# Beginning the transfers of the maxima rows from ScalarE's queue instead of SyncE's, in a two-layer fp32 transformer stack

## The reference, cut to what matters

```
x = x + attention_0(layernorm(x))   # ring attention: 16 heads of width 16, key blocks of 256
x = x + ffn(layernorm(x))           # ternary weights, relu squared
x = x + attention_1(layernorm(x))   # ordinary softmax attention, 16 heads of width 16
x = x + trees(layernorm(x))         # 8 decision trees of depth 7
```

## Time and profile before

| | |
|---|---|
| median of 3 runs | 3680.61 us (3670.45 to 3684.01) |
| the profiled execution | 3678.47 us |
| its span, first to last instruction | 3676.6 us |
| TensorE busy | 3089.0 us, 84% |
| VectorE busy | 2319.5 us, 63% |
| ScalarE busy | 1945.2 us, 53% |
| GpSimd busy | 885.4 us, 24% |
| mean granted TensorE clock | 0.914 of full speed |

### The profile page before, as it was taken

One profiled execution on the slowest core, in us unless ns is written; L12 is line 12 of the kernel. 1 busy time (PEld: TensorE's weight loads), 2 busy tenths in 40 slices (PEclk: granted clock), 3 DMA queues, 4 the chain that ended last, 5 costly groups with the idle time before them and its releaser, 6 DMA issues.

```text
span 3676.6 us, 58730 instructions
## 1 busy us (share of the span) xinstructions
PE 3089.0 (84%) x19068; PEld 1381.1 (38%) x19068; DVE 2319.5 (63%) x4191; ACT 1945.2 (53%) x2573; POOL 885.4 (24%) x1184
## 2 busy tenths in 40 slices
PE   1488898878988789788998889887898878988899
PEld 0124254232633326242452425424263332623245
DVE  0775756666576666757667575666756666676666
ACT  0273654637455464655647465473655637455563
POOL 0013132131321314122231312213132131412213
PEclk9599898979989899898999989898998979989899
DMA  3000001000100001001010000100010000100101
GB/s 110 20 20 18 20 30 34 11 18 20 40 32 2 28 21 36 26 4 34 13 42 20 18 20 24 36 15 18 20 38 33 3 27 11 47 26 2 36 14 41
DMA packets 95781, 94.49 MB, mean 26 GB/s; under 512 B 16185, under 2 KB 92761, under 8 KB 95465
## 3 DMA queue, kind: packets, MB, share of 16 engines
q1 hardware_dynamic: 87029, 82.18, 6.6%
q10 hardware_dynamic: 8448, 8.39, 0.6%
HBM read 18.66 MB, written 8.39 MB: 7 GB/s over the span
## 4 chain that ended last, share of the span: by engine, by line
issue 45%; PE 34%; POOL 9%; DVE 7%; SPq 2%; ACT 2%; DMA 1%; POOLq 0%; DVEq 0%; ACTq 0%
PE ps L957 11%; PE ps L1187 6%; PE ps L1016 5%; PE ps L994 4%; DVE nmax L727 3%; PE ps L963 2%; POOL probs L347 2%; SPq L249 2%; DVE h L705 2%; POOL parts L326 2%; POOL probs L378 1%; PE ps L1162 1%; PE ps L1005 1%; PE ps L970 1%; PE ps L1178 1%
## 5 line engine op out<-in xcount | busy, mean ns | idle before, releaser
L481 ACT ACTIVATE probs<-ps 128x1024 f32<-128x1024 f32 x1024 | 1042.8, 1026 | 422.9 <-PE ps L1005 418.9
L994 PE MATMUL ps<-kst,qst 48*128 48x512 f16 x2076 | 803.9, 436 | 268.3 <-DVE nmax L727 111.7
L724 DVE TENSOR_REDUCE nmax<-ps 128x2 f32<-128x512 f32 x1052 | 667.2, 685 | 276.9 <-PE ps L994 270.7
L727 DVE TENSOR_REDUCE nmax<-ps 128x1 f32<-128x512 f32 x1024 | 648.9, 685 | 231.9 <-PE ps L994 224.2
L1005 PE MATMUL ps<-qst,kst 54*128 54x512 f16 x2048 | 723.6, 417 | 4.0 <-ACT probs L481 4.0
L1016 PE MATMUL ps<-probs,vn 128*32 128x512 f32 x4096 | 557.7, 614 | 0.0
L994 PEld LDWEIGHTS ps<-kst,qst 48*128 48x128 f16 x2076 | 160.5, 95 | 1007.5 <-DVE nmax L727 459.4
L378 POOL TENSOR_TENSOR probs<-probs 127x512 f16<-127x512 f32 (+1 forms) x256 | 292.8, 1165 | 571.6 <-ACT probs L624 571.6
L957 PE MATMUL ps<-hT,win 128*127 128x512 f16 (+1 forms) x1536 | 357.5, 383 | 10.8 <-ACT probs L481 10.2
L1187 PE MATMUL ps<-wout,probs 127*128 127x256 f16 (+1 forms) x3072 | 357.2, 273 | 0.0
L624 ACT ACTIVATE probs<-probs 127x512 f16<-127x512 f32 (+1 forms) x256 | 161.3, 630 | 310.5 <-DVE probs L913 305.6
(11 more groups left out here) (112 smaller groups left out, 3290.8 us busy)
## 6 DMA issues: line engine op xcount, KB each, us to landing
qst<-parts SPq DMA_DIRECT2D x396, 64.0 KB, 2.6
kst<-parts SPq DMA_DIRECT2D x396, 64.0 KB, 2.6
x<-in_x SPq DMA_DIRECT2D x18, 512.0 KB, 4.7
probs<-x SPq DMA_DIRECT2D x16, 512.0 KB, 3.0
out<-probs ACTq DMA_DIRECT2D x16, 512.0 KB, 3.2
qst<-nrow SPq DMA_DIRECT2D x258, 12.0 KB
qst<-in_winT SPq DMA_DIRECT2D x1, 2040.0 KB
oT<-in_wfcT SPq DMA_DIRECT2D x1, 1024.0 KB
```

The costliest lines, as they stand in the source:

```text
L481: nc.scalar.activation(probs[:, g % 2, 2 * hf:2 * hf + 2, s % G, :], ps[:, 2 + 2 * hf:4 + 2 * hf, :], ACT.Exp).then_inc(exp_rd, 1)
L724: nc.vector.tensor_reduce(nmax[:, u, 2 * tt + half, :, slot], bank[tt % 2].rearrange("p (a s) -> p a s", s=BLK), AX.X, ALU.max, negate=Tru ...
L727: nc.vector.tensor_reduce(nmax[:, u, 2 * tt + half, 0, slot:slot + 1], bank[tt % 2], AX.X, ALU.max, negate=True).then_inc(max_rd, 1)
L994: mm(bank[tt % 2], qst[lo:hi, ai % 2, e // 2, tt * P:(tt + 1) * P], kst[lo:hi, ai % 2, e // 2, :], start=True, stop=True).then_inc(max_ps, 1)
```

## The change

ScalarE's `row_read` keeps its copy. Behind it ScalarE waits for its own count `mrow_sb`, and then begins the two transfers that SyncE began. `rows_up` is gone from SyncE's queue with all its calls. The data, the tiles, the semaphore `mstack` and TensorE's waits are the same. The calls of `row_read` are given the attention's index `ai` as well.

```
@@ sync
-            def rows_up(n, ai, g):
-                sp.wait_ge(mrow_sb, n * NG + (g + 1))
-                for half in range(2):
-                    sp.dma_start(qst[half * HALF + MROW:half * HALF + KROWS, ai % 2, 2 * g:2 * g + 2, :],
-                                 nrow[half * (ROWS // 2):(half + 1) * (ROWS // 2), g % 2, :]).then_inc(mstack[g % 2], 16)
...
@@ scalar
-            def row_read(n, g):
+            def row_read(n, ai, g):
                 act.wait_ge(mrow_ps, n * NG + (g + 1))
                 if g >= 2:
                     act.wait_ge(mstack[g % 2], n * (2 * 32) + 32 * (g // 2))
                 nc.scalar.activation(nrow[:, g % 2, :], row_bank[:, 0:S], ACT.Copy).then_inc(mrow_sb, 1)
+                act.wait_ge(mrow_sb, n * NG + (g + 1))
+                for half in range(2):
+                    act.dma_start(qst[half * HALF + MROW:half * HALF + KROWS, ai % 2, 2 * g:2 * g + 2, :],
+                                  nrow[half * (ROWS // 2):(half + 1) * (ROWS // 2), g % 2, :]).then_inc(mstack[g % 2], 16)
...
-                        row_read(*((n, (s + 2) // G) if s < 14 else (n + 1, 0)))
+                        row_read(*((n, ATT[ph], (s + 2) // G) if s < 14 else (n + 1, ATT[ph] + 1, 0)))
```

More of the change, by code:

```diff
@@ L271, in stack_up @@
                                                  parts[half * HALF:(half + 1) * HALF, part, 2 * hf + c, :]).then_inc(stack[hf], 16)
-            def rows_up(n, ai, g):
-                sp.wait_ge(mrow_sb, n * NG + (g + 1))
-                for half in range(2):
-                    sp.dma_start(qst[half * HALF + MROW:half * HALF + KROWS, ai % 2, 2 * g:2 * g + 2, :],
-                                 nrow[half * (ROWS // 2):(half + 1) * (ROWS // 2), g % 2, :]).then_inc(mstack[g % 2], 16)
             stack_up(0, 0, 0)
             stack_up(0, 0, 1)
-            rows_up(0, 0, 0)
             with sp.Fori(0, PAIRS) as b:
@@ L284, in _ @@
                     n = b * NATT + ai
-                    rows_up(n, ai, 1)
                     if ai % 2 == 0:
                         stack_up(n + 1, ai + 1, 0)
-                    rows_up(n, ai, 2)
-                    if ai % 2 == 0:
                         stack_up(n + 1, ai + 1, 1)
-                    rows_up(n, ai, 3)
-                    if ai % 2 == 0:
-                        rows_up(n + 1, ai + 1, 0)
                     if ai == 1:
@@ L306, in _ @@
                 stack_up((b + 1) * NATT, 0, 1)
-                rows_up((b + 1) * NATT, 0, 0)
             for q in range(PAIR):
@@ L506, in attention_odd @@
                     if s % G == 2 and s < 14:
-                        row_read(n, (s + 2) // G)
+                        row_read(n, ATT[ph], (s + 2) // G)
                     if s == 3:
@@ L540, in _ @@
             qk_read(0, 0, 3)
-            row_read(0, 0)
+            row_read(0, 0, 0)
             with act.Fori(0, PAIRS) as b:
@@ L586, in _ @@
                 square_high(b, 15)
-                row_read(n2, 0)
+                row_read(n2, 2, 0)
                 attention_even(b, 4)
@@ L624, in _ @@
                         nc.scalar.activation(mhi[0:rows, a % 2, leaf, :], masked[0:rows, a % 2, leaf, :], ACT.Copy).then_inc(mhi_sb, 1)
-                row_read(n4, 0)
+                row_read(n4, 0, 0)
                 send(b, 1)
```

## The result

The changed kernel took 3684.05 us (median of 20 runs), the kernel before, in 20 runs beside it, 3677.71 us. The ratio of the two is 1.0021, 95% interval 1.0011 to 1.0031: slower by 7.7 us (4.0 to 11.4), and within half a per cent; the two medians lie 6.3 us apart. The forecast had been +2.7 us, a time of 3683, range 3668 to 3718. Its class was right and the time lies in the range. The 2.7 us are about a third of what was measured and lie under the interval. The place was wrong: the two costs of which the forecast was made, 2.3 and 1.8 us, came out near nothing, and what the change costs comes from 16 sites that the prediction had put at zero.

A forecast was written before the change was run, and what follows sets the result against it. It took the ring of two banks between TensorE and VectorE as the pace in plain stretches, with ScalarE having time over. Terms 2.3 + 1.8 - 1.4 = +2.7 us gave 3683.3 as a median; range 3668 to 3718.

The forecast's parts named there:

- the two costs of which the forecast was made: 2.3 us at s = 2 of even attentions and 1.8 us at s = 10 of odd attentions, 16 sites each.
- That little was to be won: TensorE's waits for rows in qst total 3.0 us, so the gain lies between 0 and 3.0; 1.4 taken.
- the sign that was given: In the profile after, at s = 10, TensorE would show no wait for DMA.
- The stop: ScalarE's semaphore wait, two issues and restart per site: 0.03 + 1.47 + 0.25 = 1.75 us, bounds 1.43 and 2.27.
- The absorption: At s = 10 and 14 of even attentions 0.4 us of lateness is free, so the sites cost nothing.
- The point of 1.97 us: The length of ScalarE's stop past which the dense sites begin to cost.
- 48 dense sites: s = 10 and 14 of even, s = 2 of odd attentions; each said to cost nothing.
- Even s = 2: 16 sites: hT's copy behind exp (2, 1) delays VectorE's L710 by 0.14 us, 2.3 us; costs from a 1.60 stop.
- odd s = 10: 16 sites where ScalarE is the pace: exp (11, 0) 0.11 us late, 1.8 us; costs from a 1.64 stop.
- The collision of the queues: At s = 10 of even attentions ScalarE's issues wait for SyncE's: stop grows 0.96 us, +11 us, 3694; chance 0.10.
- The slower rival: The stop outgrows its cover: ScalarE loses 1 us more per site, a 2.5 stop, 52 us, 3733; chance 0.22.
- price curve: Total cost by stop length over 48, 16 and 16 sites less 1.4: 18.6 us at 2.08, 52 at 2.5.

The follow-up runs named there:

- e1: The changed kernel with the pairs at s = 2 of odd attentions begun by SyncE again, the other 113 on ScalarE; ratio to before 0.9997.
- e4: The changed kernel with three issues per site in place of two, the second transfer cut in two; ratio to before 1.0197.
- e2: The kernel before with only the 16 pairs at s = 2 of odd attentions begun by ScalarE; ratio to before 1.0025.
- e6: The changed kernel with TensorE's first transposes of oT moved from the end of s = 3 to the middle of s = 4; ratio to before 1.0004.
- e3: The changed kernel with ScalarE's wait and two issues moved behind exp (s, 1) of the same s; ratio to before 0.9990.
- e7: The kernel before with only odd s = 2 pairs on ScalarE, cut into three issues (SyncE three at even s = 2); ratio to before 1.0089.

## Why the prediction was right in its class and wrong in place

- **The time** of 3683 beside a measured 3684.05 is luck. The kernel before was taken at 3680.61 (3 runs) and is at 3677.71 in 20, and the forecast change was 2.7 us where 7.7 were measured: two costs that aren't there (4.1 us) stand for one that was put at zero (11.5 us at the sites).
- **That little was to be won** was right. The rows were waited for in 3.0 us, now in 1.8: 1.2 won, 1.4 forecast. The wait of 0.78 us of the earlier trace rows, behind SyncE's stacks, is gone. Against the sign that was given, two waits for rows of s = 10 are left, 1.05 and 0.78 us, both in phase 4; before they were 1.38 and 0.89. At both ScalarE's pair begins 0.03 us behind the copy, so no issue was held back there. Freeing SyncE's queue brought nothing else: e1, with 113 pairs moved, is at 0.9997.
- **The stop** was 1.75 in the sum, and is 1.67: wait 0.03 (0.03), pair 1.52 (1.47), restart 0.12 (0.25). The pair and the restart lay inside their bounds. The 1.47 was SyncE's figure; on ScalarE an issue takes 741 ns and not 722.
- **The absorption** at s = 10 and 14 of even attentions was right: 0.00 at a stop of 1.67. The point of 1.97 us came somewhat early: with a stop of 2.44 in e4 the sites cost 0.36 at s = 14 and 0.31 and 0.12 at s = 10, so the cost begins at 2.1 to 2.3.
- **The 16 sites at odd s = 2** are the step that failed. They were counted among the "48 dense sites" and costed by the timeline of another place, s = 14 of an even attention. Scores and maxima are alike there, and so is ScalarE's work in the next head, a copy of oT between the two exps. At s = 15 of the even attention, before the change, it is this one:

```profile
668.70 0.60 ACT L469 ACTIVATE oT<-ps 128x512 f32<-128x512 f32 x1
```

What differs is who waits for it: at odd s = 3 TensorE transposes oT at once, at even s = 15 it doesn't. The prediction asked only when the scores need the exps, and not when anyone needs the copy behind them. Its word was 0, the measure 0.72 x 16 = 11.5 us. The waits of the kernel before had the line, 4.3 us, 16 times, 0.3 us at most: too small to look like a cost, and exactly what says that there is no slack. It wasn't read.
- **Even s = 2** (2.3 us) and **odd s = 10** (1.8 us) were overrated. The first shows 0.13 and -0.09, the second 0.00. At odd s = 10 the stop, 1.71 in phase 1 and 1.67 in phase 5, is just past the point that was given, 1.64, and in e4, at 2.48 and 2.44, it costs 0.71 and 0.66, so the mechanism is there and the cost begins at about 1.78, some 0.1 us later than was said. At even s = 2 the 0.13 isn't the change's: e2, whose pair there is on SyncE, has 0.12 and -0.09 at the same sites. The lateness of VectorE is there, in all 16, and smaller than the 0.14 of the sum: from the reductions ahead of L710 (now L699) to those behind it, it is 1.80 us before and 1.90 (phase 0) and 1.85 (phase 4) after. What was wrong is that it would last: it is made up again in the heads behind; these are the heads in which TensorE also does the projections, and it probably has the pace there, which no run tried.
- **The collision of the queues** didn't happen. In the changed trace 8 of ScalarE's issues overlap one of SyncE's, by up to 0.74 us; all 8 take 0.74 us. One of them stands at 218.80:

```profile
215.07 4.35 SPq L270 DMA_DIRECT2D kst<-parts  x6
```

```profile
218.80 1.52 ACTq L453 DMA_DIRECT2D qst<-nrow  x2
```

The pair takes 1.52 us, as at s = 14. The Trainium skill ("Perfetto Trace Analysis", DMA Instruction — HWDGE) has the descriptor block locked for one sequencer at a time, with the lock wait inside the duration. By it the pair should have been longer here. These rows don't bear that out.
- **The slower rival** didn't hold: no stop between exps passes 2.08 us. Its price curve is low further up. By it a stop of 2.44 costs 48 x 0.47 + 16 x 0.84 + 16 x 0.80 - 1.4 = 47 us over before, and e4 measured 72. The curve has 0.47 us for odd s = 2, which in e4 cost 1.5 us, and with the lower clock up to 2.8; the other sites that it prices cost less than it says.

The 11.5 us of the sites and the 7.7 of the ratio just about agree: the interval of the ratio reaches from 4.0 to 11.4 us, and e2 has 9.2. The sites count somewhat high in the other runs too: e6 shows 16 x 0.42 = 6.7 us at its sites and at most 4.8 in its ratio. Part of it may lie at s = 6 of odd attentions, where the stretches at the lower clock come and go: from s = 6 to s = 9 the 16 odd attentions together take 0.4 us less after than before, and 2.0 less in e2. These are single executions, so whether the change gives back 2 to 4 us somewhere stays open.

## What to carry to other kernels

When work is put on an engine that has time over, find what stands behind it at each place of the code, not at one place per pattern, and read the short waits as well: a wait of 0.3 us that occurs every time meant here that the slack was nil, and the lateness of that copy, 0.71 us, passed through in full. A pair of transfers that ScalarE issued ahead of its next exp, behind a wait for its own result, made that exp start 1.67 us behind the copy. This cost nothing at 96 of 112 sites and 0.72 us at the 16 where somebody was waiting. Issued behind that exp, the same pair cost nothing (e3), because the exp and the idle time behind it, 1.02 and 0.53 us, covered its 1.52 us and the restart but for 0.09 us.

## What the runs showed of the hardware

- ScalarE issues the same transfer in 741 ns, SyncE in 722.
- After the last of its issues ScalarE started the next ACTIVATE in 0.12 us.
- Two queues issuing at once (SyncE and ScalarE) slowed neither, as far as the changed trace shows: 741 and 593 ns, overlapping by 0.59 us near 219 us of the span, are the durations that they have alone. Three of SyncE's overlapped issues last 1.24 to 1.90 us, but each was 0.86 us in or more when ScalarE's began, and the kernel before has 21 of over 1 us among its 792 issues of L270, with ScalarE issuing nothing beside them.
- A transfer behind an ACTIVATE that still waits for a semaphore wasn't begun until that ACTIVATE went (e3: 0.24 us after the data were ready in the timeline shown, and 5 to 7 ns behind the exp's start at all 112 sites). So ScalarE's sequencer didn't run ahead past one waiting instruction.
- Transposes of TensorE later by 0.77 us, at 16 places, were followed in 9 of them by a stretch of 3.4 us at the lower clock, 1.2 GHz, which made 0.78 us into 1.95 to 2.34 (e7). In e4 it was 9 of 16 too.
